# Softmax maxima on two 64-row tiles of TensorE, and the round reordered as maxima, value run, maxima, four scores

## What is computed

```python
x_norm = layer_norm(x, g1, beta1)
q = (x_norm @ Wq + bq).reshape(B, S, H, hd).transpose(0, 2, 1, 3)   # S = 4096, H = 16, hd = 16
k = ...; v = ...                                                     # likewise
q = apply_rope(q); k = apply_rope(k)
q = q * (1.0 / jnp.sqrt(jnp.float32(hd)))
scores = jnp.einsum('bhqd,bhkd->bhqk', q, k)
attn = jax.nn.softmax(scores, axis=-1)
out = jnp.einsum('bhqk,bhkd->bhqd', attn, v)
...
return x + _L1_attn_ref(...) + _L1_ffn_ref(...)
```

## Time and profile before

| what | us |
|---|---|
| median of 3 runs (range) | 5130.69 (5129.98 to 5139.8) |
| profiled execution, its own time | 5169.03 |
| span in the profile, first to last instruction | 5167.3 |
| busy: PE / DVE / ACT / POOL | 4621.0 / 3082.9 / 2757.2 / 355.0 |
| softmax attention stage, from POOL's first instruction in it to the last copy of `OT` | 622.2 to 3801.1 |
| mean granted clock of TensorE, as a share of 2.4 GHz | 0.931 |

### The profile page before, as it was taken

The page is one execution under the profiler, slowest core; times in us unless marked ns, Lnnn a source line. Parts: engine busy times, 40 slices in busy tenths (PEclk is TensorE's granted clock), DMA queues, the critical chain, the costliest instruction groups (busy, mean ns, idle before and its releaser), DMA issues. The chain is left out here.

```text
span 5167.3 us, 76677 instructions
## 1 busy us (share of the span) xinstructions
PE 4621.0 (89%) x23944; PEld 2069.2 (40%) x23944; DVE 3082.9 (60%) x3354; ACT 2757.2 (53%) x5129; POOL 355.0 (7%) x344
## 2 busy tenths in 40 slices
PE   6888379999999999999999999999989998667488
PEld 4666212222222222222222222222248887444355
DVE  6877377878878878878888788788501110111012
ACT  4555106777777777777777777777742222111011
POOL 1233541000000000000000000000000000000400
PEclk8988659999999999999999999999999999888699
DMA  4222490000004000013000000000035554000300
GB/s 137 78 90 78 100 183 26 2 2 2 2 8 62 1 3 2 2 18 52 2 3 2 2 3 2 3 1 1 3 124 192 192 192 161 30 24 24 110 30 20
DMA packets 215809, 254.43 MB, mean 49 GB/s; under 512 B 36224, under 2 KB 189696, under 8 KB 213760
## 3 DMA queue, kind: packets, MB, share of 16 engines
q1 hardware_dynamic: 208256, 230.68, 16.0%
q0 software_dynamic: 7296, 20.98, 1.4%
HBM read 180.57 MB, written 70.78 MB: 49 GB/s over the span
## 5 line engine op out<-in xcount | busy, mean ns | idle before, releaser
L1179 DVE TENSOR_REDUCE a_MX<-a_MP 128x1 f32<-128x1024 f32 x2048 | 2415.7, 1219 | 604.5 <-PE a_MP L1049 589.9
L1151 ACT ACTIVATE a_PT<-a_ST 128x512 f32<-128x512 f32 x4096 | 2194.6, 598 | 989.6 <-PE a_ST L1068 915.7
L1068 PE MATMUL a_ST<-a_QS,a_KS 98*128 (+1 forms) x4096 | 1403.4, 386 | 81.7 <-ACT a_PT L1151 74.4
L1049 PE MATMUL a_MP<-a_KS,a_QS 96*128 96x512 bf16 x4096 | 1271.7, 392 | 58.8 <-DMA a_KS<-scr_kparts 45.0
L1083 PE MATMUL a_OT<-a_PT,a_VG 128*32 128x512 f32 x8192 | 1115.6, 617 | 0.1
L1068 PEld LDWEIGHTS a_ST<-a_QS,a_KS 98*128 98x128 bf16 x4096 | 394.9, 97 | 1288.0 <-ACT a_PT L1151 819.5
L1049 PEld LDWEIGHTS a_MP<-a_KS,a_QS 96*128 (+1 forms) x4096 | 386.8, 99 | 543.7 <-DVE a_MX L1179 114.3
L1582 ACT ACTIVATE e_hT<-e_up,e_BF 128x256 f32<-128x256 f32 x312 | 148.0, 474 | 394.2 <-PE e_up L1535 394.0
L1083 PEld LDWEIGHTS a_OT<-a_PT,a_VG 128*32 128x32 f32 x8192 | 162.1, 108 | 428.6 <-ACT a_PT L1151 386.1
L1535 PE MATMUL e_up<-e_xT,e_WF 128*128 128x256 f32 x1248 | 322.2, 381 | 0.8 <-DVE e_xT L1592 0.8
L1544 PE MATMUL e_dn<-e_WP,e_hT 128*128 128x256 f32 x1248 | 321.0, 380 | 0.0
(11 more groups left out here) (205 smaller groups left out, 2774.5 us busy)
## 6 DMA issues: line engine op xcount, KB each, us to landing
e_WF<-Wfc SPq DMA_DIRECT2D x39, 1024.0 KB, 4.9
e_WP<-Wproj SPq DMA_DIRECT2D x39, 1024.0 KB, 7.1
a_QS<-scr_qparts SPq DMA_DIRECT2D x192, 64.0 KB, 13.8
a_KS<-scr_kparts SPq DMA_DIRECT2D x24, 512.0 KB, 18.0
scr_xs<-f_zero SPq DMA_DIRECT2D x1, 9984.0 KB, 32.8
e_XS<-scr_xs SPq DMA_DIRECT2D x39, 256.0 KB, 2.7
scr_ys<-e_Y SPq DMA_DIRECT2D x39, 256.0 KB, 2.2
f_X<-x SPq DMA_DIRECT2D x16, 512.0 KB, 4.6
```

The lines of the kernel that those rows point to most:

```text
L1049: last = T.matmul(MP[:, slot, i, :], QS[j][0:ROWS, bass.ds((b * HG + h) * BLK + t * P, P)], KS[j][0:ROWS, h, (kb + i) * BLK:(kb + i + 1) * ...
L1068: T.matmul(ST[:, bank_of(c), :], KS[j][:, h, u * P:(u + 1) * P], QS[j][:, bass.ds((b * HG + h) * BLK, BLK)], start=True, stop=True).then_i ...
L1151: nc.scalar.activation(PT[:, c % RING, :], ST[:, bank_of(c), :], ACT.Exp, scale=SOFT_SCALE).then_inc(S["exp_done"], 1)
L1179: V.reduce_max(MX[:, x:x + 1], MP[:, slot, :, :].rearrange("p a n -> p (a n)"), AX.X).then_inc(S["mp_free"], 1)
```

## The change

Three things change in `attention`.

- **Layout.** `KS` and `QS` get 128 rows. Each head belongs to a side (heads 0 and 1 of a group to side 0, heads 2 and 3 to side 1). Four of the six products of a head (64 rows) lie in its side's half of the rows, the two others and the shifts in the other half; the rest of a window of 32 rows is ones in `KS` and zeros in `QS`. A score matmul contracts all 128 rows. Each load is split into two of half the size (109 instead of 55 per group), and so is the DMA of the shifts. POOL sets eight regions instead of two before it makes the identity.
- **Maxima.** The two matmuls of a pair now contract 64 rows each: one head of side 0 on rows 0 to 63, one head of side 1 on rows 64 to 127. They leave out the two smallest products, so the shift is a near-maximum; softmax does not depend on it. VectorE reduces a pair to two columns instead of one. There are 64 pairs per block as before.
- **Order.** In a round PE issues a pair, the value run, a pair, and then four scores in a row. The PE loop over blocks 0 to 5 of a group is written out.

```diff
+HALF = 64
+LEADING = HALF // HD1
+SIDES = HG // 2
-PAIRS = HG * TPB * KB // 2
+PAIRS = HG // 2 * TPB * KB
...
+def main_row(side, r):
+    return HD1 * r + HALF * side if r < LEADING else HD1 * (r - LEADING) + HALF * (1 - side)
+def shift_row(side):
+    return HALF * (1 - side) + HD1 * (len(Q_PART) - LEADING)
...
             for j in range(2):
-                nc.gpsimd.memset(KS[j][ROWS:STACK, :, :], 1.0).then_inc(S["ones_ok"], 1)
-                pool.wait_ge(S["ones_ok"], j + 1)
+                for side in range(SIDES):
+                    r0, h0 = shift_row(side), side * HS
+                    nc.gpsimd.memset(KS[j][r0:r0 + WIN, h0:h0 + HS, :], 1.0).then_inc(S["ones_ok"], 1)
+                    nc.gpsimd.memset(QS[j][r0:r0 + WIN, :].rearrange("r (b h n) -> r b h n", b=NB, h=HG)[:, :, h0:h0 + HS, :],
+                                     0.0).then_inc(S["ones_ok"], 1)
+            pool.wait_ge(S["ones_ok"], 4 * SIDES)
...
             def load_k(G, r, sem):
-                heads = slice(G * HG * HD1, (G + 1) * HG * HD1)
-                sp.dma_start(KS[G % 2][HD1 * r:HD1 * (r + 1), :, :], scr["kparts"][K_PART[r], heads, :].rearrange(
-                    "(h e) n -> e h n", e=HD1)).then_inc(sem, 16)
+                for side in range(SIDES):
+                    h0, row = G * HG + side * HS, main_row(side, r)
+                    sp.dma_start(KS[G % 2][row:row + HD1, side * HS:(side + 1) * HS, :],
+                                 scr["kparts"][K_PART[r], h0 * HD1:(h0 + HS) * HD1, :].rearrange(
+                        "(h e) n -> e h n", e=HD1)).then_inc(sem, 16)
...
             def max_pair(e, slot, j, b, x):
-                for i in range(2):
-                    last = T.matmul(MP[:, slot, i, :], QS[j][0:ROWS, bass.ds((b * HG + h) * BLK + t * P, P)],
-                                    KS[j][0:ROWS, h, (kb + i) * BLK:(kb + i + 1) * BLK], start=True, stop=True)
+                for side in range(SIDES):
+                    hs, half = side * HS + h, slice(side * HALF, (side + 1) * HALF)
+                    last = T.matmul(MP[:, slot, side, :], QS[j][half, bass.ds((b * HG + hs) * BLK + t * P, P)],
+                                    KS[j][half, hs, kb * BLK:(kb + 1) * BLK], start=True, stop=True)
...
                         if x % 2 == 0:
-                            score(n, j, b, HG * u + SBANKS)
                             if u:
                                 weigh(n, j, u - 1)
...
-                            if u < KT - 1:
-                                score(n, j, b, HG * u + SBANKS + 1)
-                    if u < KT - 1:
-                        score(n, j, b, HG * u + SBANKS + 2)
-                        score(n, j, b, HG * u + SBANKS + 3)
+                    for c in range(HG * u + SBANKS, min(HG * (u + 1) + SBANKS, CHUNKS)):
+                        score(n, j, b, c)
...
             pe.wait_ge(S["ident_ok"], 1)
-            pe.wait_ge(S["ones_ok"], 2)
...
-                with pe.Fori(0, NB - 2) as b:
+                for b in range(NB - 2):
                     one_block(G, b, (j, b + 1), (j, b + 2))
...
             def maximum(e, slot, x):
-                V.reduce_max(MX[:, x:x + 1], MP[:, slot, :, :].rearrange("p a n -> p (a n)"), AX.X).then_inc(S["mp_free"], 1)
+                V.tensor_reduce(MX[:, :, x], MP[:, slot, :, :], AX.X, ALU.max).then_inc(S["mp_free"], 1)
```

More of the change, by code:

```diff
@@ L918, in attention @@
         load = (S["load0"], S["load1"])
[L919 to L923, removed]
+        LOADS = SIDES * (NB + 1) * len(Q_PART) + 1
+        FIRST = SIDES * 2 * len(Q_PART)
+        HS = HG // SIDES
+        KS = [sb(f"KS{j}", [P, HG, N_TOK], bf16) for j in range(2)]
+        QS = [sb(f"QS{j}", [P, NB * HG * BLK], bf16) for j in range(2)]
         VG = [sb(f"VG{j}", [P, KT, HG * 2 * HD1]) for j in range(2)]
         PT = sb("PT", [P, RING, BLK])
-        MX = sb("MX", [P, PAIRS])
+        MX = sb("MX", [P, SIDES, PAIRS])
         neg = sb("neg", [P, HG * TPB])
-        negparts = sb("negparts", [P, SHIFTS, HG * TPB], bf16)
+        negparts = sb("negparts", [P, SIDES, SHIFTS, HS * TPB], bf16)
         negT = sb("negT", [SHIFTS * HG * TPB, P], bf16)
@@ L979, in load_q @@
             def load_q(G, r, b, sem):
-                heads = slice(G * HG * HD1, (G + 1) * HG * HD1)
-                sp.dma_start(QS[G % 2][HD1 * r:HD1 * (r + 1), b * HG * BLK:(b + 1) * HG * BLK].rearrange(
-                    "e (h n) -> e h n", h=HG), scr["qparts"][Q_PART[r], heads, b * BLK:(b + 1) * BLK].rearrange(
-                    "(h e) n -> e h n", e=HD1)).then_inc(sem, 16)
-            def load_k(G, r, sem):
-                heads = slice(G * HG * HD1, (G + 1) * HG * HD1)
-                sp.dma_start(KS[G % 2][HD1 * r:HD1 * (r + 1), :, :], scr["kparts"][K_PART[r], heads, :].rearrange(
-                    "(h e) n -> e h n", e=HD1)).then_inc(sem, 16)
+                for side in range(SIDES):
+                    h0, row = G * HG + side * HS, main_row(side, r)
+                    heads, c0 = slice(h0 * HD1, (h0 + HS) * HD1), (b * HG + side * HS) * BLK
+                    sp.dma_start(QS[G % 2][row:row + HD1, c0:c0 + HS * BLK].rearrange(
+                        "e (h n) -> e h n", h=HS), scr["qparts"][Q_PART[r], heads, b * BLK:(b + 1) * BLK].rearrange(
+                        "(h e) n -> e h n", e=HD1)).then_inc(sem, 16)
+            def load_k(G, r, sem):
+                for side in range(SIDES):
+                    h0, row = G * HG + side * HS, main_row(side, r)
+                    sp.dma_start(KS[G % 2][row:row + HD1, side * HS:(side + 1) * HS, :],
+                                 scr["kparts"][K_PART[r], h0 * HD1:(h0 + HS) * HD1, :].rearrange(
+                        "(h e) n -> e h n", e=HD1)).then_inc(sem, 16)
             def load_v(G, sem):
@@ L1008, in store_negmax @@
                 sp.wait_ge(S["negmaxT_copied"], n + 1)
-                sp.dma_start(QS[j][ROWS:STACK, bass.ds(b * HG * BLK, HG * BLK)], negT[:]).then_inc(S["negmax_load"], 16)
+                for side in range(SIDES):
+                    rows = SHIFTS * HS * TPB
+                    sp.dma_start(QS[j][shift_row(side):shift_row(side) + SHIFTS, bass.ds((b * HG + side * HS) * BLK, HS * BLK)],
+                                 negT[side * rows:(side + 1) * rows, :]).then_inc(S["negmax_load"], 16)
             def store_out(n, G, b):
@@ L1017, in _ @@
             load_group(1)
+            sp.wait_ge(S["ones_ok"], 4 * SIDES)
             store_negmax(0, 0, 0)
@@ L1044, in max_pair @@
             def max_pair(e, slot, j, b, x):
-                h, t, kb = x // (TPB * KB // 2), x // (KB // 2) % TPB, x % (KB // 2) * 2
+                h, t, kb = x // (TPB * KB), x // KB % TPB, x % KB
                 room(e)
-                for i in range(2):
-                    last = T.matmul(MP[:, slot, i, :], QS[j][0:ROWS, bass.ds((b * HG + h) * BLK + t * P, P)],
-                                    KS[j][0:ROWS, h, (kb + i) * BLK:(kb + i + 1) * BLK], start=True, stop=True)
+                for side in range(SIDES):
+                    hs, half = side * HS + h, slice(side * HALF, (side + 1) * HALF)
+                    last = T.matmul(MP[:, slot, side, :], QS[j][half, bass.ds((b * HG + hs) * BLK + t * P, P)],
+                                    KS[j][half, hs, kb * BLK:(kb + 1) * BLK], start=True, stop=True)
                 last.then_inc(S["mp_full"], 1)
@@ L1071, in score_first @@
             def score_first(n, j, b):
-                pe.wait_ge(S["negmax_load"], 16 * (n + 1))
+                pe.wait_ge(S["negmax_load"], 16 * SIDES * (n + 1))
                 for c in range(SBANKS):
@@ L1122, in _ @@
             negmax_transpose(PAIRS, PAIRS % 2, 0)
+            pe.wait_ge(S["ones_ok"], 4 * SIDES)
             pe.wait_ge(load[0], (LOADS - FIRST) * 16)
```

14 lines of the change are left out of this document (7 added, 7 removed).

## The result

| | median of the runs | lowest to highest |
|---|---|---|
| before, same chip | 5134.66 us (4 runs) | 5129.98 to 5139.80 |
| changed | 5328.39 us (4 runs) | 5322.90 to 5333.76 |

The changed kernel is slower: its time is 1.0377 times that of before, with an interval of [1.0359, 1.0395], or 194 us more. The forecast was 5370 us, 240 more. On another chip (experiment 9) the two kernels gave 1.0383 [1.0361, 1.0406]. The profiled execution took 5333.76 us (span 5332.0), 5 above its median.

The account below looks back on a forecast made before the run. PE's order and work were taken as the bound. The median 5130.7 us plus 222 for 31 blocks and 18 for the start gave 5370 us, with a range of 5285 to 5530.

Parts of the forecast that it names:

- What bounds the kernel: Attention's ordinary round of 2.83 us: PE's order and work set the pace; VectorE and ScalarE have 0.5 to 0.7 us spare.
- The maxima matmuls: A pair's two matmuls run side by side, 0.22 us instead of 0.44, removing 0.44 us of PE work per round.
- Mode changes: PE's tiling changes per round go from two to four; each added one costs 0.11 us, between 0.08 and 0.20.
- The order: Four scores on three banks: the fourth waits for the first's exponential, 1.08 us; round 3.06 us instead of 2.83.
- A block: Sum over a block's 32 steps: 7.2 us more, times 31 blocks with maxima, 222 us.
- (a): The 29 ordinary steps of a block: 0.225 us more each, 6.5 us together.
- (b): The last step of a block: 2.95 us instead of 2.19, +0.76.
- (c): Block boundary: PE's 4.57 us until ScalarE stays; the first value run then follows after 0.65 us instead of 0.97, -0.32.
- (d): Half clock for 3 us behind a block boundary, where pair and chain are longer: +0.2 us, an estimate.
- PE's loop written out: Writing out PE's block loop is worth nothing, since the stall at the boundary is ScalarE's.
- The start: Fills doubled to 55.1 us, PE begins at about 679 instead of 656.5, shift wait gone: net +18 us, bounds 0 and 25.
- Loads and shifts: Twice as many DMAs with the same bytes: costed at nothing; otherwise three or four blocks could each lose a few us.

Follow-up runs that it names:

- experiment 9: Kernel before, changed kernel and that of experiment 4, all unchanged, rerun on one chip: 5138.14, 5336.57 (ratio 1.0383) and 4988.52 us (0.9705).
- experiment 3: Changed kernel with the last of the four scores moved behind the next round's first pair, ahead of the value run: 5055.54 us, ratio 0.978 to before.
- experiment 4: Changed kernel reordered to value run, three scores, both pairs together, fourth score: 5017.41 us, ratio 0.9698 to the kernel before.
- experiment 5: Kernel before with only PE's block loop written out: 5136.12 us, ratio 0.9989 to the kernel before.
- experiment 2: Changed kernel with the order of before, so the 64-row tiles alone: 5129.57 us, ratio 0.9918 to the kernel before.
- experiments 7 and 8: Experiment 4's kernel with ScalarE's block loop written out (4973.20 us, ratio 0.967 to before), then also the identity made ahead of GpSimd's fills (4952.99 us, 0.9631).

## Why the prediction was right, and where its size was off

**What bounds the kernel.** Right. PE's order sets the pace, and the rounds followed PE's starts in all kernels: 2.83, 3.04, 3.26, 2.82, 2.72 and 2.62 us.

**The maxima matmuls.** Right: two on 64 rows each last as long as one. This was read off a run on tiles of 32 rows.

**Mode changes.** 0.11 was taken, between 0.08 and 0.20. Measured are 0.10 in three of the four places of the round, 0.13 out of the value run, and 0.10 between experiments 3 and 4. The 0.20 did not come back anywhere, so leaning to the lower of the two ends was right. The reason given for it, the weights that follow, was not tried.

**The order.** Right, and this is the term that decides. From first to fourth score it is 1.08 as forecast, and experiment 3 shows by moving one score that it is this wait. The round is 3.04 for 3.06.

**A block.** The forecast was 7.2 us more, and 5.7 was measured. The steps one by one, for a block with the fall of the clock in both kernels, where the difference is 6.2 (means of 18 blocks of the changed kernel and 27 of the one before):

- (a) Ordinary steps: 29 x 0.225 = 6.5 forecast, 5.9 measured. The new round is 3.04 instead of 3.06. And 2.83 was taken for all steps of before, which is a little low: 12 rounds give 2.835, and of the steps next to the shifts two take 3.08 and 3.05, against a single one of 3.44 in the changed kernel. This makes 27 x 3.04 + 3.44 against 26 x 2.835 + 6.13, or 5.7, and 0.26 for the step with the output's transpose (3.63 for 3.37).
- (b) The last step: 2.95 forecast, 2.93 measured.
- (c) The boundary: the wait of 4.57 "stays", and is 4.62 at the boundary shown; the first run 0.65 after it, measured 0.64. Right within 0.05.
- (d) Half clock: +0.2 was an estimate. Measured is a gain of about 0.15: the step behind the boundary takes 4.24 for 4.30, and the fall makes the boundary's own step 0.10 longer (5.32 for 5.22) where it made it 0.19 longer before. PE has less to do there now, which would explain it; this was not tried. And in a third of the blocks the clock did not fall at all, which is worth another 1.3 us each. This was not in the sum.

So the mechanism was right, and the mis-sized term is the one per block: 31 x 1.4, or 43 us too much, nearly the whole difference between 240 and 194. Of the 1.4 some 0.6 is (a), 0.35 is (d), where the sign was wrong, and 0.45 the blocks without a fall (10 of 29 by 1.3).

**PE's loop written out** is worth nothing: right within 0.2%, 0.9989 in experiment 5.

**The start.** +18 was forecast, with PE at 679, the fills doubled to 55.1 us and the wait for the shifts gone. Measured: PE at 676.13, 56.9 us behind the first fill, no wait for the shifts, and 18.7 us up to the first exp (experiment 9). The size is right, but half by luck. PE's first pair comes 22.8 us later there, and 4.1 of these come back, though not from the wait of 4.47 for the shifts: the undisturbed kernel before has no such wait (its first scores start behind the 12 pairs without idle time). Most of the 4.1 comes from VectorE, whose pairs the forecast left at 1.18 us each. Before (experiment 9), and changed:

```profile
656.68 75.31 DVE L1179 TENSOR_REDUCE a_MX<-a_MP 128x1 f32<-128x1024 f32 x64 [35.62 <-PE a_MP L1049]
676.77 72.50 DVE L1200 TENSOR_REDUCE a_MX<-a_MP 128x2 f32<-128x1024 f32 x64 [58.03 <-PE a_MP L1074]
```

The 64 reductions take 2.8 us less with two results each, and the 12 behind them 0.45 less (13.67 for 14.12). From start to start it is 1.13 us for 1.18. Two errors of nearly the same size cancelled: a wait that belonged to one disturbed execution, and a pace of VectorE that did not stay.

**Loads and shifts.** Costed at nothing. Right: no block of the changed kernel stands out, and SyncE's halves of `QS` are issued in about half the time each. The 84 loads at the start take 39.59 us, 0.47 each, for 42 in 37.13. Loading all of group 2 takes 54.2 us for 42.8:

```profile
630.49 39.59 SPq L999 DMA_DIRECT2D a_QS<-scr_qparts  x84
```

**The base of the sum.** The differences were added to the median and not to the profiled execution. This was right. Against the profile of experiment 9 that execution was 31 us longer: 5 between the first fill and the first exp, 17 in the first block, 10 behind the attention, and nothing in the 31 blocks from which the rounds were read. Added to 5169 the sum would have been off by twice as much.

**The rivals.** "The wait is hidden and PE's work decides" would be 2.61 per round and 4951 us. It fell for this order, at 1.08 in each round. But experiment 4, with its round of 2.62 us, is this rival made true by an order that fills the wait. Beside the kernel before it saved 152 us (4988.52 for 5140.06 in experiment 9), where the rival had 180; the steps in which VectorE is the limit, among others, were not in its sum. "Added changes of mode are free", "the pairs run one after the other" and "dearer than 0.20" fell with the same rows. The clock stayed at 1.00 in mid-block, at 2.17 us of computing in 3.04.

## What to carry to other kernels

Where an accumulator ring of k banks feeds another engine, k+1 writes in a row put the whole round trip (write, read by the other engine, release) on the path wherever it is longer than the k writes, here 1.08 us against 0.65. Look for it in a stretch where other work is missing, because it is exposed there already, and put the work that is left between the k-th and the next write. A stall that stands in front of everything can be worth little: ScalarE's 2.1 us per block brought 0.3, since VectorE was as late. And before adding differences to a profile, see how far its own time is from the median, and where.

## What was not expected of the hardware

- A change of mode costs nearly the same between any two of the full array, 64-row tiles and 32-column tiles: 0.10 us in three places of the round (and 0.10 from a score into the value run in experiment 4), 0.13 out of the value run.
- GpSimd's fill of 32 rows of 8192 elements takes 6.92 us, and that of 2 rows of 16384 took 13.8. Between 2 and 32 rows the number of rows made no difference; both are 0.84 ns per element of a row.
- TensorE's granted clock fell to 0.50 (1.2 GHz) behind a boundary with an idle stretch of 2.33 us, and stayed at 1.00 behind another with 2.26, in one profile of one kernel. A fall costs 1.3 us per block here and some 1.7 in the kernel before, by the two lengths of their blocks. Of 29 blocks the clock fell in 28 in the kernel before, 19 in the changed one, 13 in experiment 2, 20 in experiment 3, 1 in experiment 4 (6 when repeated) and none in experiments 7 and 8. What decides whether it falls was not tried.
- VectorE's reduction of 1024 columns with two results instead of one takes 1226 ns for 1219 by itself, but 1.13 us for 1.18 from start to start when many stand in a row.
